# A graph layer with residual and layer norm: one of three ring loads of each group issued by ScalarE instead of SyncE

## The reference

```python
agg = A_hat @ (X @ W_agg)                       # A_hat 8192x8192 f32, X 8192x64
out = w[:, None] * relu(agg) + (1.0 - w)[:, None] * X
return layernorm(X + out)                       # over the 64 columns, eps 1e-5
```

## Time and profile before

| | |
|---|---|
| median of 3 runs | 638.98 us (638.19 to 639.09) |
| the profiled execution | 637.91 us |
| its span | 636.0 us |
| PE busy | 507.3 us, 80% of the span |
| ACT busy | 15.3 us |
| DMA | 272.76 MB, mean 429 GB/s |
| SP's queue (q1) | 99.5% of 16 engines' span |
| share of DMA in the chain that ended last | 74% |
| mean granted TensorE clock | 0.929 |

### The profile page before, as it was taken

The page is one execution under the profiler, slowest core; times in us unless marked ns, Lnnn a source line. Parts: engine busy times, 40 slices in busy tenths (PEclk is TensorE's granted clock), DMA queues, the critical chain, the costliest instruction groups (busy, mean ns, idle before and its releaser), DMA issues.

```text
span 636.0 us, 7548 instructions
## 1 busy us (share of the span) xinstructions
PE 507.3 (80%) x3456; PEld 238.2 (37%) x3456; DVE 52.2 (8%) x112; ACT 15.3 (2%) x41; POOL 0.3 (0%) x6
## 2 busy tenths in 40 slices
PE   0395987987987896896987796977996896898996
PEld 0142433433433442442433442433443343343445
DVE  2000100200100100100020110020020020020102
ACT  0000000000000000000000000000000000000000
POOL 0000000000000000000000000000000000000000
PEclk9997989989989999999899989899889889798999
DMA  9999999999999999999999999999999999999998
GB/s 366 432 431 450 431 432 450 418 448 407 431 434 446 439 427 450 403 462 407 437 429 446 440 425 439 413 456 414 442 424 446 426 439 432 421 433 428 425 422 350
DMA packets 7796, 272.76 MB, mean 429 GB/s; under 512 B 1264, under 2 KB 1520, under 8 KB 2032
## 3 DMA queue, kind: packets, MB, share of 16 engines
q1 hardware_dynamic: 7488, 272.63, 99.5%
q10 hardware_dynamic: 304, 0.07, 0.0%
HBM read 270.60 MB, written 2.10 MB: 429 GB/s over the span
## 4 chain that ended last, share of the span: by engine, by line
DMA 74%; PE 25%; SPq 0%; issue 0%; DVE 0%; ACT 0%; DVEq 0%
DMA ring<-adj_main_dram 69%; PE bank L179 22%; DMA ring<-adj_mid_dram 4%; PE bank L169 2%; PE bank L187 0%; SPq L120 0%; ACT aggT L239 0%; SPq L116 0%; SPq L115 0%; SPq L141 0%; DVE res L298 0%; ACT std_last L229 0%; DVE y_last L292 0%; ACT aggT L242 0%; DVE stats L294 0%
## 5 line engine op out<-in xcount | busy, mean ns | idle before, releaser
L179 PE MATMUL bank<-ring,x_sb 128*64 128x512 f32 (+1 forms) x3072 | 461.8, 464 | 113.5 <-DMA ring<-adj_main_dram 113.5
L179 PEld LDWEIGHTS bank<-ring,x_sb 128*64 128x64 f32 x3072 | 207.0, 146 | 366.6 <-issue 246.3
L276 DVE SCALAR_TENSOR_TENSOR y<-bank,w_sb 128x320 f32<-128x320 f32 (+1 forms) x13 | 6.3, 481 | 557.7 <-PE bank L187 557.7
L169 PE MATMUL bank<-ring,x_sb 128*64 128x384 f32 (+1 forms) x256 | 28.5, 381 | 0.1
L187 PE MATMUL bank<-wagg,aggT 128*128 128x64 f32 x128 | 17.3, 280 | 11.2 <-ACT aggT L234 10.3
L187 PEld LDWEIGHTS bank<-wagg,aggT 128*128 128x128 f32 x128 | 15.3, 191 | 15.0 <-ACT aggT L234 13.2
L169 PEld LDWEIGHTS bank<-ring,x_sb 128*64 128x64 f32 x256 | 15.8, 137 | 12.1 <-issue 9.6
L233 ACT COPY aggT<-bank 128x512 f32<-128x512 f32 x12 | 7.0, 585 | 531.7 <-PE bank L179 531.7
L265 DVE TENSOR_TENSOR y<-y,res 128x320 f32<-128x320 f32 (+1 forms) x13 | 6.3, 482 | 1.7
L273 DVE TENSOR_TENSOR res<-y,rstd 128x320 f32 (+1 forms) x13 | 6.3, 482 | 0.4
L267 DVE SCALAR_TENSOR_TENSOR y<-rowsum,y 128x320 f32<-128x320 f32 (+1 forms) x13 | 6.3, 482 | 0.4
(11 more groups left out here) (13 smaller groups left out, 2.3 us busy)
## 6 DMA issues: line engine op xcount, KB each, us to landing
ring<-adj_main_dram SPq DMA_DIRECT2D x23, 7040.0 KB, 34.6
ring<-adj_main_dram SPq DMA_DIRECT2D x12, 6400.0 KB, 37.2
ring<-adj_mid_dram SPq DMA_DIRECT2D x1, 4224.0 KB, 29.3
ring<-adj_main_dram SPq DMA_DIRECT2D x1, 3840.0 KB, 25.9
ring<-adj_main_dram SPq DMA_DIRECT2D x1, 3200.0 KB, 33.1
ring<-adj_mid_dram SPq DMA_DIRECT2D x1, 3072.0 KB, 21.3
ring<-adj_mid_dram SPq DMA_DIRECT2D x1, 2304.0 KB, 26.4
x_sb<-x_dram SPq DMA_DIRECT2D x1, 2048.0 KB, 8.3
```

What stands on the lines that cost most here:

```text
L169: last = nc.tensor.matmul(into[j % 2 * D:(j % 2 + 1) * D, 0:cols], x_sb[:, j], ring[:, at + s * cols:at + (s + 1) * cols], start=j < 2, st ...
L179: last = nc.tensor.matmul(into[half * D:(half + 1) * D], x_sb[:, j], ring[:, at + c0:at + c1], start=j < 2, stop=j >= T - 2)
L276: step(nc.vector.scalar_tensor_tensor(out=y[:, 0:n], in0=rows.rearrange("p (n d) -> p n d", d=D), scalar=0.0, in1=over_row(w_sb[:, bass.ds ...
```

## The change

SP issues (g,0) and (g,1) of the groups 1 to 10, and no longer (g,2). ACT issues (g,2) for these ten groups, on its own queue. Its loop now waits at its head for `slot_free >= g * C`, which is the release of (g-1,2), copies the sums of group g-1, issues (g,2), and then takes the root of group g-1. Group 0 and group 11 are issued by SP alone, as before. The two last turns of ACT's loop are written out.

```diff
+        def main_load(engine, c, load, first, end, landed):
+            j, at = sum(MAIN_LOADS[:c]), c * SLOT
+            engine.dma_start(ring[:, at + first * COLS:at + end * COLS],
+                             load[:, :, j + first:j + end].rearrange("o q s n -> (o q) (s n)")).then_inc(landed, 16)
...
             with sp.Fori(1, G - 1) as g:
-                for c in range(C):
+                for c in range(C - 1):
                     sp.wait_ge(slot_free, g * C + (c + 1 - C))
-                    main_load(c, adj_main[bass.ds(g, 1), 0], 0, MAIN_LOADS[c], loaded[c])
+                    main_load(sp, c, adj_main[bass.ds(g, 1), 0], 0, MAIN_LOADS[c], loaded[c])
...
-            with act.Fori(0, G) as g:
-                act.wait_ge(slot_free, g * C + C)
+            def copy_sums():
                 nc.scalar.copy(aggT[:, 0:BANK], acc).then_inc(agg_copied, 1)
                 nc.scalar.copy(aggT[:, BANK:COLS], acc_rest).then_inc(agg_copied, 1)
+
+            def root_of(g):
                 std_of(std[:], varsum[:], 1.0 / D, g * DVE_GROUP + (DVE_PRE + VAR_STEP))
                 act.wait_ge(out_ready, g + 1)
+
+            with act.Fori(1, G - 1) as g:
+                act.wait_ge(slot_free, g * C)
+                copy_sums()
+                main_load(act, C - 1, adj_main[bass.ds(g, 1), 0], 0, MAIN_LOADS[C - 1], loaded[C - 1])
+                root_of(g - 1)
+            for g in (G - 2, G - 1):
+                act.wait_ge(slot_free, g * C + C)
+                copy_sums()
+                root_of(g)
```

More of the change, by code:

```diff
@@ L116, in _ @@
             sp.dma_start(w_sb[:], w.rearrange("(p t) -> p t", p=P)).then_inc(w_in, 16)
[L117 to L121, removed]
             for c in range(C):
-                main_load(c, adj_main[0:1, 0], 0, MAIN_LOADS[c], loaded[c])
+                main_load(sp, c, adj_main[0:1, 0], 0, MAIN_LOADS[c], loaded[c])
             with sp.Fori(1, G - 1) as g:
-                for c in range(C):
+                for c in range(C - 1):
                     sp.wait_ge(slot_free, g * C + (c + 1 - C))
-                    main_load(c, adj_main[bass.ds(g, 1), 0], 0, MAIN_LOADS[c], loaded[c])
+                    main_load(sp, c, adj_main[bass.ds(g, 1), 0], 0, MAIN_LOADS[c], loaded[c])
             for c in range(C):
@@ L132, in _ @@
                 whole = MAIN_LOADS[c] - (REST if c == C - 1 else 0)
-                main_load(c, adj_main[G - 1:G, 0], 0, whole, loaded[c])
-            main_load(C - 1, adj_main[G - 1:G, 0], whole, whole + REST, rest_loaded)
+                main_load(sp, c, adj_main[G - 1:G, 0], 0, whole, loaded[c])
+            main_load(sp, C - 1, adj_main[G - 1:G, 0], whole, whole + REST, rest_loaded)
             j, freed = 0, 0
```

## The result

The changed kernel takes 640.39 us (median of 22 runs, 638.95 to 642.05) against 637.89 us before (median of 22, 637.50 to 640.22): 2.5 us more by the medians. The ratio is 1.0033, interval 1.0025 to 1.0041. It is slower by a third of a per cent. The forecast was 642.0, which is 3.0 us on top of the 638.98 of the three runs then shown; the larger set puts the kernel before 1.1 us lower, so the sizes to compare are 3.0 and 2.5. The profiled execution took 639.16 us, its span is 637.4 us, so it is one of the quicker ones: 1.25 us above the one profiled before, where the medians are 2.5 us apart.

What follows compares the result with a forecast made beforehand. The prediction took the kernel as bound by DMA, with PE nearly binding at the end. All terms were 0 but 3.0 us for PE's late tail, which on the 638.98 us shown gave 642.0, range 638.3 to 647.5.

Steps and rivals of the forecast that it cites:

- The order of the bytes: Loads of groups 1 to 10: engines serve both queues row by row, so (1,1) lands at 104.2, not 90.4.
- Rival A: Ring loads: engines finish a begun load before turning to the other queue; order unchanged, 0.0 us; 0.26 with the tail absorbing it.
- The time of ACT's issue: ACT's loop: (g,2) goes out after the copies, 1.3 us later than by SP; by itself this costs 0.
- Do the engines run dry?: DMA engines in groups 1 and 2: no, 3.3 us to spare in group 1; last byte at 630.6 as before.
- The pattern: From group 2 on: (g,2) lands 8.4 us later than now, about 8.2 us before (g+1,0), and this repeats.
- The tail: From (10,2), landing at 551.1, to the last contraction: PE ends at 634.3 against 631.3, 3.0 us later.
- B: DMA engines: two streams are slower than one; at 1% per row 3.8 us more, some 645.8; chance 0.12.
- C: DMA engines: ACT's queue gets less than half; engines dry 7.7 us a group, up to 77 us; chance 0.06.
- D: DMA queues: two queues hide what lies between transfers; at most 2 us faster, 637.0; chance 0.06.
- The sum: Whole kernel: only the 3.0 us at the end count, 640.9 from the profiled execution, 642.0 from the median shown.

Runs made afterwards that it cites:

- the kernel with the late first issue: Changed kernel, but ACT issues (1,2) behind the root of group 0, 6.5 us later: 639.86 us, 1.9 us slower than before the change.
- the one with the last two loads: Kernel before, but ACT issues (9,2) and (10,2) alone: 639.33 us, ratio 1.0009.
- (10,2) alone: Kernel before, but ACT issues only (10,2) and SP all other loads: 642.38 us, ratio 1.0056.
- the same order made by SP's queue: Kernel before, with group 10's second and third loads cut into parts and issued in turn by SP alone: 643.07 us, ratio 1.0082.
- nine loads: Kernel before, but ACT issues (1,2) to (9,2), SP (10,2) and the rest: 639.31 us, ratio 1.0015.

## Why the prediction was right, point by point

**The order of the bytes.** Right in kind: rows of the two queues alternate. If whole loads had taken turns in the old order, (1,1) would have landed at 90.4; had (1,2) passed it whole, (1,2) would have landed near 92, and it landed at 107.8. The stretches of 2 us show the turns themselves, 16 rows of one queue, then 16 of the other. Rival A is out. The Trainium skill (DMA: Bandwidth & Descriptors, Queues, rings and completion order) has an engine turn between rings packet by packet, with some 9 to 17 descriptors in a packet. The turns agree, if a packet is what the profile counts as one, a single row; rival A's reading, 8 rows and a completion in one turn, does not hold for these loads.

**The time of ACT's issue.** A step that was wrong. The forecast had it wait for the copies and 0.5 us more, 1.3 us in all; it went out at 72.71, 0.2 us behind PE's end at 72.50 and 0.16 us after the first copy had begun, and took 0.36 us, and the second copy began at 73.03 while it was out. With 72.7 + 3.5 = 76.2 in place of 78.1 the same working has 7.6 rows of (1,2) in front of (1,1)'s end, 15.7 us, and (1,1) at 106.2; the forecast said 104.2, and 107.16 was measured. The last 1.0 us is in what the working left out: the engines are not in step, two of them being a turn behind, and a completion waits for a turn like a row.

**Do the engines run dry?** Wrong too, and from the same slip. With (1,1) at 107.2, (1,1)'s slot is free at 119.9 and its next load effective at 123.4, when what is outstanding lasts to 123.7: the 3.3 us to spare were 0.3, not enough for all 16 engines, and their share was 0.53 from 120 to 122. The forecast had 0 here and the last byte at 630.6; it landed at 631.6.

**The pattern.** (g,2) was forecast 8.4 us later than before; it was 9.4 (164.80 against 155.44) in group 2 and 9.3 in group 10. The forecast waits of about 17 and 8 us were 19.71 and 7.73.

**The tail.** (10,2) at 551.1 was forecast, 552.11 measured; three other kernels had 551.00, 551.03 and 551.08. The last contraction was forecast at 634.3 and ended at 632.65 in this execution, because (10,2) ran at full speed, 12.06 us, after a wait of 3.14 us. The pattern had slipped in groups 4 and 10, where the waits were 4.01 and 2.96, 4.18 and 3.14, in place of 0.3 to 1.8 and 7.7. The short wait alone does not explain the full speed: (4,2) took 14.97 us after its 2.96. From (10,2)'s start to the end PE took 80.5 us here; in the kernel with the late first issue, where (10,2) took 15.05, it took 83.5, against the 83.2 of the forecast, and ended at 634.55, 4.0 us behind the last landing. So the tail as forecast was seen, but in that trace and in the one with the last two loads; in the changed kernel's own trace the gap is 1.0 us. That its typical run, 1.2 us longer than this one, has the tail of those two is argued, not shown. The slip may differ from run to run, which would explain why the six runs with (10,2) alone spread over 3.3 us and those with the same order made by SP's queue over 1.3; that too is argued.

**The other rivals.** B is out: the stretches give 433 and 434 GB/s with both queues in use, and the price per load failed with (10,2) alone (0.2 against 4.5 us) and with nine loads (2.0 against at most 1.7). C did not occur, as the shares are equal. D is out, as the kernel is slower.

**The sum.** The forecast put 3.0 us to PE's backlog in the tail and nothing to the engines. In the execution profiled the engines lost 1.0 us and PE's end moved by 1.3; of the 2.5 us between the medians some 1.5 us are left for the tail, half of the forecast term, if the engines lose as much in a typical run, which no trace shows. So the order of the bytes, its delay of 8 to 9 us and the place where it is paid were right, and that 2.5 came so near to 3.0 is in part luck: a term too large and one left out nearly made up for each other.

## What to carry to other kernels

Where the DMA engines are never idle, a second queue moves no more bytes; it changes their order, and the load needed next shares the engines with the one needed after it. In a ring that lands later, frees its slot later, and is paid where the consumer has least slack: the same switch cost 0.4 us, not clear of none, in the middle of this kernel and 4.5 us in its last group but one. So ask of a moved transfer what it will now run beside, which wanted load it delays, and whether the consumer can still catch up before the last byte.

## What the runs showed of the hardware that was not expected

- A DMA that stands behind both of ACT's copies in program order was issued while the first ran (72.71 against 72.55 to 73.13) and 0.32 us before the second began, and did not hold it up: the two copies began 0.48 us apart, as before the change (73.30 and 73.78).
- Two queues share the engines row by row and evenly, 16 rows of one queue between 80 and 82 us and 16 of the other between 82 and 84: SP's load of 6.6 MB had just begun when ACT's of 7.2 MB came in, and they landed 0.7 us apart.
- PE's slot of 22 slices took 13.4 to 15.07 us after waits of 7.7 us, but 12.06 us after one of 3.14 and 14.97 after one of 2.96; the granted clock was 0.79 over the stretch with the wait of 19.71 us.
